# At an odd sequence's end, the next chunk's value transposes and a part of the maxima's matmuls move ahead of the outputs' burst

## The reference

```python
x = x + 0.5 * ffn(_layernorm(x), W_up, W_gate, W_down)
x = x + attn(_layernorm(x), Wq, bq, Wk, bk, Wv, bv)
x = x + 0.5 * ffn(_layernorm(x), W_up, W_gate, W_down)

def ffn(x, W_up, W_gate, W_down):      # each W: scale * clip(round(W / scale), -1, 1)
    return (silu(x @ wu.T) * (x @ wg.T)) @ wd.T      # 256 -> 1024 -> 256

def attn(x, ...):                      # 16 heads of 16, 4 key/value groups
    q, kg, vg = einsum(x, Wq) + bq, einsum(x, Wk) + bk, einsum(x, Wv) + bv
    scores = einsum('bhqd,bhkd->bhqk', q, k) / sqrt(16)
    attn = softmax(where(causal, -inf, scores))
    return einsum('bhqk,bhkd->bhqd', attn, v).transpose(0, 2, 1, 3).reshape(...)
```

## Time and profile before

| | us |
|---|---|
| median of 3 runs | 584.15 (583.83 to 584.58) |
| the profiled execution | 583.65 |
| its span, first to last instruction | 581.9 |
| TensorE busy | 554.8 (95%) |
| VectorE busy | 480.2 (83%) |
| ScalarE busy | 399.2 (69%) |
| GpSimd busy | 168.5 (29%) |
| chain that ended last | TensorE 77%, VectorE 15%, ScalarE 3% |

### The profile page before, as it was taken

The page is one execution under the profiler, slowest core; times in us unless marked ns, Lnnn a source line. Parts: engine busy times, 40 slices in busy tenths (PEclk is TensorE's granted clock), DMA queues, the critical chain, the costliest instruction groups (busy, mean ns, idle before and its releaser), DMA issues.

```text
span 581.9 us, 12392 instructions
## 1 busy us (share of the span) xinstructions
PE 554.8 (95%) x4244; PEld 343.9 (59%) x4244; DVE 480.2 (83%) x1862; ACT 399.2 (69%) x716; POOL 168.5 (29%) x264
## 2 busy tenths in 40 slices
PE   2989999999999989999999999998999999999998
PEld 2445556656566756666566666554455656656566
DVE  6898978998875889999999998996897688666664
ACT  5857655765745469798888888887665765765642
POOL 3115201101440033555556463666301101110100
PEclk9999999999999999999999999999999999999999
DMA  8711101100104161323323323221302211111112
GB/s 304 235 30 37 19 19 37 37 20 19 38 0 116 34 148 58 90 73 85 102 52 103 85 67 85 69 50 39 38 1 58 52 55 55 37 56 55 36 37 73
DMA packets 72222, 37.90 MB, mean 65 GB/s; under 512 B 35520, under 2 KB 71616, under 8 KB 72128
## 3 DMA queue, kind: packets, MB, share of 16 engines
q1 hardware_dynamic: 72160, 37.11, 24.7%
HBM read 18.22 MB, written 10.49 MB: 49 GB/s over the span
## 4 chain that ended last, share of the span: by engine, by line
PE 77%; DVE 15%; ACT 3%; issue 2%; POOL 2%; DMA 1%; DVEq 0%; ACTq 0%; POOLq 0%
PE bank L1178 33%; PE bank L1190 17%; DVE sm_out L994 6%; PE bank L1339 5%; PE bank L1282 5%; PE bank L1309 5%; PE bank L1350 5%; PE bank L1364 2%; PE bank L1355 2%; PE bank L1154 1%; DVE hid L858 1%; DVE stats L738 1%; POOL xn L415 1%; ACT shared L598 1%; DVE hl L873 1%
## 5 line engine op out<-in xcount | busy, mean ns | idle before, releaser
L488 ACT ACTIVATE silu<-bank,w_scale 128x512 f32<-128x512 f32 x128 | 87.3, 683 | 114.1 <-PE bank L1178 114.1
L994 DVE CUSTOM_DVE_ANT_0 sm_out<-bank,mask 128x256 f16<-128x256 f32 (+1 forms) x512 | 151.0, 351 | 12.3 <-PE bank L1309 11.6
L858 DVE SCALAR_TENSOR_TENSOR hid<-silu,h_unit,bank 128x512 f32<-128x512 f32 x128 | 95.0, 743 | 63.5 <-ACT silu L488 63.1
L1190 PE MATMUL bank<-wT_down,hh 128*128 128x256 f16 x512 | 118.3, 273 | 2.5 <-DVE hl L873 2.3
L1190 PE MATMUL bank<-wT_down,hl 128*128 128x256 f16 x512 | 118.2, 272 | 0.0
L1178 PE MATMUL bank<-xh,wT_up 128*128 128x512 f16 x256 | 98.0, 383 | 1.1 <-DVE xl L802 0.7
L873 DVE TENSOR_TENSOR hl<-hid,hh 128x512 f16<-128x512 f32 x128 | 98.8, 772 | 0.0
L1178 PE MATMUL bank<-xh,wT_gate 128*128 128x512 f16 x256 | 97.3, 380 | 1.0 <-DVE hid L858 1.0
L1178 PE MATMUL bank<-xl,wT_up 128*128 128x512 f16 x256 | 98.0, 383 | 0.0
L1178 PE MATMUL bank<-xl,wT_gate 128*128 128x512 f16 x256 | 97.3, 380 | 0.0
L424 POOL TENSOR_TENSOR xnl<-xn,xnh 128x1024 f16<-128x1024 f32 x13 | 28.3, 2176 | 211.0 <-ACT xn L527 177.8
(11 more groups left out here) (134 smaller groups left out, 795.1 us busy)
## 6 DMA issues: line engine op xcount, KB each, us to landing
q_st<-q_scratch SPq DMA_DIRECT2D x32, 256.0 KB
q_scratch<-q_hl SPq DMA_DIRECT2D x16, 256.0 KB, 2.3
out_dram<-x SPq DMA_DIRECT2D x7, 512.0 KB, 3.0
x<-in_x_dram SPq DMA_DIRECT2D x1, 3072.0 KB, 15.5
k_scratch<-k_hl SPq DMA_DIRECT2D x16, 128.0 KB, 2.4
k_st<-k_scratch SPq DMA_DIRECT2D x16, 128.0 KB
x<-in_x_dram SPq DMA_DIRECT2D x2, 512.0 KB, 4.3
shared<-in_w_up_t_dram SPq DMA_DIRECT2D x2, 512.0 KB, 6.5
```

What stands on the lines that cost most here:

```text
L488: act.activation(silu[:, e % 2, :], U[e % 2][:, :], ACT.Silu, scale=w_scale[:, 0:1]).then_inc(silu_ready, 1)
L858: dve.scalar_tensor_tensor(out=hid[:, e % 4, :], in0=silu[:, e % 2, :], scalar=h_unit[:, 0:1], in1=GT[e % 2][:, :], op0=ALU.mult, op1=ALU. ...
L994: ins = dve.tensor_tensor_reduce(sm_out[:, i, cols], SM[i][:, cols], mask[:, S - size:S], -1.0 / MAX_UNIT, -MASKED, ALU.add, ALU.min, rowm ...
L1190: ins = pe.matmul(ACC[t % 2][:, 0:D], part[:, par, e, t * P:(t + 1) * P], wT_down[:, e, :], start=(e == 0 and part is hh), stop=(e == NE - ...
```

## The change

In TensorE's stream, at an odd sequence's end, `val_transposes` of the next chunk and part 0 of `max_scores` for the group seven ahead move from behind the burst to in front of the wait for `mx_ready` and the burst. `scores` of the group two ahead (part 0) and the output transposes stay behind the burst. No instruction is added or removed, no wait's count changes, and the other engines' streams stay as they are. At the last pair's k = 1 only the matmuls of `max_scores` move.

```diff
                         elif g % 2:
                             if last and k == 2:
                                 scores(*second, range(0, 2))
+                            if odd and g == 3:
+                                if not last:
+                                    val_transposes(c + 2, (onorm_ready, 2 * b + 1))
+                                max_scores(n + 7, k + 2, 2, range(0, 1))
                             pe.wait_ge(mx_ready, 2 * (b + 1) + g // 2 + 1)
                             outputs((n - 1, n), k)
-                        if odd and g == 3 and not last:
-                            val_transposes(c + 2, (onorm_ready, 2 * b + 1))
                         projection(3)
                         if odd and g == 3:
                             if not end:
-                                max_scores(n + 7, k + 2, 2, range(0, 1))
                                 scores(*second, range(0, 1))
                                 output_transposes(b, k, 0, (onorm_ready, 2 * b + 2))
                                 output_transposes(b, k, 1, (onorm_ready, 2 * b + 1) if last else (val_ready, c + 3))
```

## The result

The changed kernel takes 588.29 us (median of 4 runs, 588.15 to 588.57), against 584.19 us for the kernel before in the same comparison: ratio 1.0071, 95% interval 1.0058 to 1.0084. The forecast was 588.0, range 586.0 to 589.4. The page after differs little in its totals: the span is 4.9 us longer (581.9 before), and TensorE's share is still 95%, since the instructions are the same and the new idle time is spread thin (30.8 us not busy in the span, against 27.1).

A forecast was written before the change was run, and what follows sets the result against it. The prediction took TensorE's stream as the path at odd ends; six delays of 0.61 us and one of 0.21 made 3.87 us over the 584.15 us median, forecast 588.0, range 586.0 to 589.4.

The forecast's parts named there:

- Part 1: Ahead of the burst: only the weight loader idles, so moved work hides at most 0.02 us per place; nothing taken.
- A to T: Odd end, from the last score matmul to the output transposes: 2.60 us before, the latter 0.61 later at six ends.
- Part 2: In front of the burst: value transposes 0.39 us, maxima's matmuls 0.21 streamed; inputs ready, nothing taken for exposed weights.
- A to V: From the last score matmul to the value transposes in front: 0.22 us, or 0.10 more if their weights are exposed.
- Part 3: Burst to output transposes: ScalarE's copy keeps 1.18 us round trip, TensorE stands 0.63; +0.61 at six ends, +0.21 at seventh.
- V, M and S just fill it: Before, value transposes, maxima's matmuls and early score matmul exactly cover the 1.18 us from burst's last group to output transposes.
- Part 4: VectorE at k = 3: its 0.43 us wait for the maxima goes, but normalisation is about 0.61 later; worth nothing.
- Does it reach the end: Odd-end delays pass on in full where the chain crosses to VectorE, which waits 0.79 us there; all taken.
- The sum: Over odd ends: 6 x 0.61 + 0.21 = 3.87 us, from a median of 584.15 to 588.0 us.
- Faster, because the burst's wait is real: Real array idle before the burst gets filled and VectorE's gaps fill: 581.1 to 582.4 us; 6%.
- Half is absorbed: Delays of one kind of odd end (k = 3) vanish: 2.0 us, so 586.2; 12%.
- more than the sum: Late normalisation also holds up L1154, or ScalarE's exponential a score matmul: 1.4 to 2.1 us more, 589.4 to 590.1; 11%.

The follow-up runs named there:

- M alone in front: Against the kernel before, only the two max_scores matmuls move in front of the burst, val_transposes stay behind it: 586.23 us, ratio 1.0034.
- The split copy: ScalarE's copy of the burst at odd ends split into two of 256 columns: 586.91 us on the changed kernel, 583.93 us on the kernel before.
- The filled gap: Changed kernel with 0.43 us of later max_scores and scores work put ahead of the output transposes: 588.24 us, 0.05 less.

## Why the prediction was right, step by step

- **Part 1 (nothing to hide ahead of the burst): held.** With M alone in front, at k = 3 and at the seventh end, A to T grew by 0.23, all that M costs; had a wait stood ahead of the burst, M would have gone into it. After the change the list of waits names L591 in 12 cases instead of 19, and "issue" in 13 instead of 7, for idle stretches of nearly the same sum (6.9 and 7.2 us).
- **Part 2 (V and M in front cost nothing but their place): one term mis-sized.** I gave A to V 0.22, with S as the nearest row, and kept the exposed weights for the upper bound. It is 0.31 at k = 1 and 0.32 at k = 3; S is a full-height matmul, V has 64 rows. That 0.10 is the larger part of the distance between 0.61 forecast and 0.72 measured. M's readout was in time, as worked out, but only because V is ahead of it; alone it waits 0.24 at k = 1.
- **Part 3 (the uncovered copy): held to the hundredth.** The round trip stayed 1.18, the gap 0.63, and the seventh end cost 0.22. The split copy shows by intervention that the copy is on the path after (1.38 us) and not measurably before (0.07). "V, M and S just fill it" left out 0.05 that the late load of T's weights costs; it is there in both orders (T takes 0.93 in both) and so takes nothing from the sum.
- **Part 4 (VectorE gains nothing): held in the result.** The 0.43 at k = 3 became 1.18 before the reciprocal (266.16), 0.76 at k = 1. My "some 1.0" and "0.6" were 0.2 low, of which the 0.10 is V's. I said that the normalisation and L1154 are late together and stopped there; the runs showed that they are tied, and that TensorE waits 0.12 for the second normalisation in either order. This took nothing from the sum, since both orders have it, but it made the picture "TensorE's empty time is the loss" wrong as a cause. The filled gap won nothing.
- **Does it reach the end: held.** The period grew by 1.45 us, both odd ends' delay in full; VectorE's 0.79 us at the crossing is still there (245.95). I had named 54.8 us for the period, and it is 55.02.
- **The sum** was 3.87 and would have been 4.5 with V's weights, which is what the traces give (4.54); the medians give 4.10. Two misses of opposite sign, 0.7 (mostly the weights) and 0.4 between the traces and the medians, make the forecast look closer than its terms: that 588.0 came within 0.3 us of 588.29 is in part luck. The 0.4 stays open but for the last pair's scatter of 0.3.
- **Rivals.** "Faster, because the burst's wait is real" fell with M alone in front: more work was ahead of the burst and nothing came back. "Half is absorbed" fell with the period. Of "more than the sum", the mechanism (L1154 held up by the normalisation) exists with 0.12 but is no addition to the change.

## What to carry to other kernels

Before moving work out from behind a producer, look at who uses the producer's result next and how long the way over the other engine is: here 1.18 us from the burst's last group to the transposes, covered to within some 0.07 us by just what was moved away. An idle bracket ahead of an instruction, and the name in it, show a wait of the array only if the starts of the matmuls around it are further apart than at a place where nothing could be waited for. And an empty stretch on the busiest engine is not the loss if the next thing after it hangs on the same chain: fill it in a trial, and see whether the gap only moves.

## What the runs showed of the hardware

- The change of form has a price on TensorE: a packed burst (128x32 weights) behind a full 128x128 matmul starts 0.10 us later than the array's time (0.31 to 0.33 where 0.21 is streamed), and so do the transposes with 64-row weights (0.31 to 0.32 behind one matmul of 512 columns or two of 256). On the way out of the burst it is the same: 0.33 to 0.34 from its last group to V, M or S, against 0.22 from such a group to the next one inside the burst. Between V and the burst, both of other forms, none shows beyond V's 0.39.
- ScalarE's copy of 512 columns out of PSUM takes 0.60 us and the way burst, copy, matmul 1.18. In two copies of 256 columns (0.66 together) the way over the first of them is 0.91.
- A group of eight transposes that the timeline shows as one busy piece of 1.16 us can hold a wait of 0.12 us; the distance to the next matmul tells (1.00 against 0.88).
